# Attention score products as four 32-key column tiles, with the second half of the tokens reversed

## What is computed

```python
q = rope(h @ Wq)              # 32 heads of 64
k = rope(h @ Wk)              # 8 groups of 64, each shared by 4 heads
scores = q @ k.T              # per head, 256 queries x 256 keys
scores = (scores - slope * abs(i - j)) / 8
scores = 30 * tanh(scores / 30)
scores = where(j <= i, scores, -inf)       # causal
probs = softmax(scores)
ctx = probs @ v
x = x + ctx @ Wo + bo
```

## Time and profile before

| what | value |
|---|---|
| timed runs, median | 1184.27 us (1182.19, 1184.27 and one of 4972.99) |
| span of the profiled execution, first to last instruction | 1182.6 us |
| what lies around the span, by the median | 1.7 us |
| mean granted TensorE clock | 0.995 of full |
| PE busy | 1146.9 us (97%) |
| DVE, POOL, ACT busy | 877.6, 688.9, 554.0 us |
| attention stage, from the first scores to the last | 39.1 to 647.8 us |

### The profile page before, as it was taken

How to read it: one execution, slowest core, us unless ns; L and a number is a source line. 1 busy time by engine, 2 the same in 40 slices (tenths; PEclk the granted TensorE clock), 3 DMA queues, 4 the chain that set the end, 5 groups by cost and what they waited for, 6 DMA issues and landing times. The chain is left out here.

```text
span 1182.6 us, 24878 instructions
## 1 busy us (share of the span) xinstructions
PE 1146.9 (97%) x9715; PEld 794.2 (67%) x9730; DVE 877.6 (74%) x1287; ACT 554.0 (47%) x617; POOL 688.9 (58%) x557
## 2 busy tenths in 40 slices
PE   4888999999999999999999999999999999999998
PEld 4655556657657566566565677777886776786683
DVE  6879878787888787878887688889745745654654
ACT  6766565564755656647556400000244543542441
POOL 1454395784865957849659589999342422423331
PEclk9999999999999999999999999999999999999999
DMA  9563443554445335543455367772012022012000
GB/s 324 156 201 116 121 131 111 164 188 117 125 146 173 122 123 167 187 120 120 129 174 186 116 124 148 143 150 67 1 20 48 7 55 54 18 35 54 19 19 36
DMA packets 166142, 133.48 MB, mean 113 GB/s; under 512 B 69628, under 2 KB 127362, under 8 KB 166082
## 3 DMA queue, kind: packets, MB, share of 16 engines
q1 hardware_dynamic: 141128, 126.44, 36.3%
q10 hardware_dynamic: 24960, 6.29, 3.6%
HBM read 81.76 MB, written 35.21 MB: 99 GB/s over the span
## 5 line engine op out<-in xcount | busy, mean ns | idle before, releaser
L700 PE MATMUL bank<-hT_halves,w_hi 128*128 128x256 f16 x640 | 176.2, 275 | 5.4 <-DVE hT_halves L1419 3.6
L1973 POOL TENSOR_TENSOR parts<-parts 128x512 f32<-128x512 f32 x80 | 118.8, 1489 | 106.8 <-DVE parts L1435 106.8
L701 PE MATMUL bank<-hT_halves,w_hi 128*128 128x256 f16 x640 | 175.8, 275 | 0.0
L702 PE MATMUL bank<-hT_halves,w_lo 128*128 128x256 f16 x640 | 175.8, 275 | 0.0
L952 PE MATMUL bank<-kv,toep 128*128 128x288 f32 (+2 forms) x660 | 159.5, 404 | 0.7 <-ACT qT L1200 0.5
L1978 POOL TENSOR_SCALAR_AFFINE_SELECT region_c<-region_c 128x512 f32<-128x512 f32 x128 | 113.2, 908 | 63.5 <-ACT region_c L1166 63.3
L952 PEld LDWEIGHTS bank<-kv,toep 128*128 128x128 f32 x660 | 124.7, 192 | 34.4 <-ACT qT L1200 0.8
L2121 POOL TENSOR_TENSOR sqsum<-sqsum,toep 128x512 f32<-128x512 f32 x56 | 78.0, 1393 | 95.5 <-ACT toep L1342 95.3
L1991 POOL TENSOR_TENSOR ctx_lo<-ctx,ctx_hi 128x512 f16<-128x512 f32 x64 | 99.0, 1547 | 59.1 <-ACT ctx_hi L1142 59.1
L1163 ACT ACTIVATE region_c<-bank,cap_scale 128x1536 f32<-128x1536 f32 x64 | 98.7, 1542 | 74.2 <-PE bank L768 73.6
L1031 PE MATMUL bank<-odd_halves,guT 128*128 128x256 f16 x512 | 112.2, 273 | 0.0
(11 more groups left out here) (192 smaller groups left out, 2666.4 us busy)
## 6 DMA issues: line engine op xcount, KB each, us to landing
unit_halves<-halves SPq DMA_DIRECT2D x80, 256.0 KB, 2.2
q_both<-unit_halves SPq DMA_DIRECT2D x64, 256.0 KB, 2.9
q_high<-unit_halves SPq DMA_DIRECT2D x64, 128.0 KB, 3.0
toep<-kernel_padded SPq DMA_DIRECT2D x32, 256.0 KB, 3.9
wffn<-w_gu SPq DMA_DIRECT2D x6, 1280.0 KB, 6.2
cpair<-ctx_pairs SPq DMA_DIRECT2D x32, 176.0 KB, 4.8
xin<-x SPq DMA_DIRECT2D x8, 512.0 KB, 3.9
region_o<-wq SPq DMA_DIRECT2D x4, 1024.0 KB, 11.3
```

What stands on the lines that cost most here:

```text
L700: pe.matmul(dst, lh, rh, start=first and k == 0, stop=False)
L701: pe.matmul(dst, lh, rl, start=False, stop=False)
L702: mm = pe.matmul(dst, ll, rh, start=False, stop=last and k == n - 1)
L1973: pool.tensor_tensor(slot[:, 0], slot[:, 0], slot[:, 1], ALU.add).then_inc(unit_summed, 1)
```

## The change

Three things, all within `scores`, `mask` and the host's preparation.

1. Each bank is computed by four column tiles of 32 keys: tile c of a bank holds keys 32c to 32c + 31 of the bank's block and writes partitions 32c to 32c + 31. For each bank first the four high products are issued (L779 in the new numbering), then the four low ones (L781). That is 24 matmuls for a group where there were 6.
2. A tile takes only the queries that can see its keys. In banks 0 and 1 tile c takes the queries from 32c on: 512, 448, 384 and 320 columns for c = 0 to 3 (two heads). The rest of the bank holds what was there, is passed through tanh and exp as before, and is zeroed by the mask.
3. The last 128 tokens stand in reverse order everywhere (inputs, rotary tables, bias, context and output are permuted on the host). So in bank 2 the queries that can see a key stand before it, and tile c takes the first 32(c + 1) of them: 128, 256, 384 and 512 columns (four heads). Over the three banks each tile has 1152 columns in its high and 1152 in its low products. The mask of bank 2 has its signs turned.

Tiles are issued from c = 3 down to 0.

```diff
+KW = 32
...
-                def both(dst, t, heads, queries):
-                    keys = slice(t * P, (t + 1) * P)
-                    pe.matmul(dst, k_high[:, g, keys], q_both[:, heads, queries], start=True, stop=False)
-                    return pe.matmul(dst, k_low[biased, g, keys], q_high[biased, heads, queries], start=False, stop=True)
-
-                for n in range(2):
-                    both(bank[:, SC_BANKS[n], :], 0, slice(REP * g + 2 * n, REP * g + 2 * n + 2), slice(0, S))
-                both(bank[:, SC_BANKS[2], :], 1, slice(REP * g, REP * (g + 1)), slice(P, S)).then_inc(sc_filled, 1)
+                def score_tiles(n):
+
+                    for c in reversed(range(P // KW)):
+                        own, keys = slice(c * KW, (c + 1) * KW), slice(n // 2 * P + c * KW, n // 2 * P + (c + 1) * KW)
+                        if n < 2:
+                            yield (bank[own, SC_BANKS[n], :].rearrange("p (h s) -> p h s", h=2)[:, :, c * KW:], keys,
+                                   slice(REP * g + 2 * n, REP * g + 2 * n + 2), slice(c * KW, S))
+                        else:
+                            yield (bank[own, SC_BANKS[n], :].rearrange("p (h s) -> p h s", h=REP)[:, :, 0:(c + 1) * KW], keys,
+                                   slice(REP * g, REP * (g + 1)), slice(P, P + (c + 1) * KW))
+
+                for n in range(3):
+                    for dst, keys, heads, queries in score_tiles(n):
+                        pe.matmul(dst, k_high[:, g, keys], q_both[:, heads, queries], start=True, stop=False)
+                    for dst, keys, heads, queries in score_tiles(n):
+                        mm = pe.matmul(dst, k_low[biased, g, keys], q_high[biased, heads, queries], start=False, stop=True)
+                mm.then_inc(sc_filled, 1)
...
-                for s in (sc_first[:, g % 3, :, 0:P], sc_second[:, g % 3]):
-                    last = pool.affine_select(s, s, pattern=[[0, REP], [1, P]],
-                                              compare_op=ALU.is_ge, fill=0.0, base=0, channel_multiplier=-1)
+                for s, sign in ((sc_first[:, g % 3, :, 0:P], 1), (sc_second[:, g % 3], -1)):
+                    last = pool.affine_select(s, s, pattern=[[0, REP], [sign, P]],
+                                              compare_op=ALU.is_ge, fill=0.0, base=0, channel_multiplier=-sign)
...
+TOKENS = np.concatenate([np.arange(0, P), np.arange(S - 1, P - 1, -1)])
+HEADS = TOKENS[::HD] // HD
```

More of the change, by code:

```diff
@@ L2149, in _ @@
             inverse_rms(B - 1)
+TOKENS = np.concatenate([np.arange(0, P), np.arange(S - 1, P - 1, -1)])
+HEADS = TOKENS[::HD] // HD
 def shape_constants():
     inv_freq = (1.0 / np.float32(10000.0) ** (np.arange(0, DH, 2, dtype=np.float32) / np.float32(DH))).astype(np.float32)
-    freqs = inv_freq[:, None] * np.arange(S, dtype=np.float32)[None, :]
+    freqs = inv_freq[:, None] * TOKENS.astype(np.float32)[None, :]
     cos = np.repeat(np.cos(freqs).astype(np.float32), REP, axis=0) * np.float32(QK_DOWN)
@@ L2162, in pieces @@
         return [a, b, (v - a - b).astype(np.float16)]
-    at = np.arange(S, dtype=np.float64) - S // 2
+    at = TOKENS.astype(np.float64) - S // 2
     slopes = np.array(SLOPES, dtype=np.float64)[:, None] * BIAS_SCALE * np.ones(S)
@@ L2186, in by_halves @@
         return np.asarray(w).reshape(NG, REP, 2, SQ, D).transpose(0, 2, 1, 3, 4).reshape(NH * DH, D)
-    c = np.asarray(ctx_2048).reshape(B, HM, HD, LB, P).transpose(1, 4, 3, 0, 2)[:, ::-1]
+    c = np.asarray(ctx_2048)[:, TOKENS].reshape(B, HM, HD, LB, P).transpose(1, 4, 3, 0, 2)[:, ::-1]
     c = np.concatenate([c, c[..., 0:WRAP - HD]], axis=-1).reshape(HM, P, LB * B, WRAP)
@@ L2191 @@
     arrays = {
-        "x": x, "ctx_pairs": c, "wq": by_units(L0_attn_Wq), "wk": by_units(L0_attn_Wk), "wv": L0_attn_Wv, "wo": by_halves(L0_attn_Wo),
-        "bo": L0_attn_bo, "kern": L0_xattn_ssm_kernel, "dcoef": L0_xattn_D, "w_gu": L0_ffn_w_gate_up, "w_p": L0_ffn_w_proj,
+        "x": np.asarray(x)[:, TOKENS], "ctx_pairs": c, "wq": by_units(L0_attn_Wq), "wk": by_units(L0_attn_Wk), "wv": L0_attn_Wv, "wo": by_halves(L0_attn_Wo),
+        "bo": L0_attn_bo, "kern": np.asarray(L0_xattn_ssm_kernel)[HEADS], "dcoef": np.asarray(L0_xattn_D)[HEADS], "w_gu": L0_ffn_w_gate_up, "w_p": L0_ffn_w_proj,
         "rope_cos": cos, "rope_sin": sin, "key_bias": key_bias, "query_bias": query_bias, "ident": ident,
@@ L2201 @@
     r = run_bass_kernel_spmd(nc, [arrays], core_ids=[0])
-    return r.results[0]["out"]
+    return np.asarray(r.results[0]["out"])[:, TOKENS]
```

## The result

| | before | after |
|---|---|---|
| median | 1184.12 us (four runs, one of them 4972.99) | 1196.24 us (four runs, 1191.5 to 1199.93) |
| ratio to before, 95% interval | | 1.0107, 1.0075 to 1.0139 |
| span of the profiled execution | 1182.6 us | 1192.8 us |
| mean granted TensorE clock | 0.995 | 0.991 |
| first scores to first scores, batches 0 to 7 | 96.8, then 78.6 to 78.9 six times | 95.1, 80.5, 84.8, 81.1, 81.6, 80.1, 77.2 |

A forecast was written before the change was run, and what follows sets the result against it. PE was taken to bound the loop, with POOL's ctx_lo close behind. Gains of 3.6 us in the loop, 0.6 in batch 0 and 0.1 in batch 7 made 4.3, so 1180.0 us, range 1171 to 1187.

The forecast's parts named there:

- What is late next: Loop, other engines: their work stays; POOL's ctx_lo holds PE at step 7, leaving 0.60 us a batch.
- the sum for PE alone: PE's own gain from cheaper scores: 1.94 us a batch, 15.5 us over eight batches, the most possible.
- 1.00 us a group: Scores of a group on column tiles: four tiles overlap fully, 1.00 us instead of 1.30.
- issue order: Rival, scores: a tile's product waits until the one issued before has started; 1.11 us a group, 1181.6 us; chance 0.18.
- float16 tiles in each other's way: Slower rival, scores: four float16 streams can't run together; over 1.30 us a group, about 1222 to 1350 us; chance 0.08.
- slow weight loads: Scores: if a tile takes weights no faster than 0.11 us a pass, a group takes 1.09 us.
- 0.11 us in and 0.12 out between full array and tiles: PE's changes between full array and column tiles: 0.11 us going in, 0.12 us going back.
- PE busy down by about 14 us: Sign that the forecast is right: PE's busy time falls by about 14 us.
- A wait of 1.3 us for ctx_lo at step 7: Sign in each loop batch: PE newly waits about 1.3 us for POOL's ctx_lo before its step 7 filler.
- The small one at step 5: Loop batches: perhaps also a small new wait of PE for ctx_lo at step 5, no size given.
- 4.3 us in all: Whole kernel: 3.6 us from six loop batches, 0.6 from batch 0 and 0.1 from batch 7.
- 0.6 for batch 0: Batch 0, not bound by PE: 0.6 us gained of a possible 1.9, from scores on the queries' chain.

The follow-up runs named there:

- e8: Changed kernel with the value products left out in the loop as in e7, and the low score products of three of four tiles too; 1179.94 us, ratio 0.9974.
- e2: Changed kernel with PE's loop of batches 1 to 6 written out, so without jumps back; 1185.88 us, ratio 1.0024.
- e7: Kernel before, with only the first of four heads' second value products (keys 128 to 255) made in the loop; 1184.37 us, ratio 1.001.
- e3: Kernel before with PE's loop of batches 1 to 6 written out, so without jumps back; 1187.36 us, ratio 1.0033.
- e13: The kernel of e6 with its loop unchanged, but full score products in groups 0 to 2 of batch 0; 1199.24 us, ratio 1.013.
- e6: Changed kernel with column tiles in the loop only in groups 6 and 7, full score matmuls in the other groups; 1181.64 us, ratio 0.9987.
- e9: Changed kernel with, in the loop, tiles of 32 keys in groups 6 and 7, of 64 in group 5, full matmuls elsewhere; 1180.83 us, ratio 0.9979.
- e14: Changed kernel with, in the loop, tiles of 32 keys only in groups 5 to 7, and full products in group 0 of batch 0; 1181.89 us, ratio 0.9986.
- e4: Changed kernel with two column tiles of 64 keys instead of four of 32; 1208.66 us, ratio 1.0197.
- e10: The kernel of e9 with tiles of 64 keys in the loop's groups 4 and 5 too; 1207.56 us, ratio 1.0218.
- e12: The kernel of e10 with the same loop, but full score products in group 0 of batch 0; 1181.13 us, ratio 0.9987.
- e1: Kernel before with each full score product cut into four of 128 columns on the full array; 1202.61 us, ratio 1.0166.
- e15: Kernel before with its loop unchanged, but full score products of groups 0 to 3 of batch 0 cut into four; 1202.84 us, ratio 1.0177.

## Why the prediction was wrong, and what of it held

**The step that failed** is the sentence under "What is late next" that says "no DMA changes, so nobody else gets less to do", and with it the sum for PE alone, which priced PE's own 144 matmuls more a round by their columns. A DMA did change: the queue of PE's instructions went from no packet in the loop to 44, with five waits on issue, 11.6 us in all. That PE's instructions have to be brought, and that the loop was held at the engine until then, was no term of the sum and no rival. It could have been seen: the page of before gives the instruction queue 37 packets for the whole program, and the DMA view of the loop has none of them. What was lacking is a count of the loop's instructions and of the pieces they touch.

The account of the loop: six batches at the forecast's 78.1 us are 468.6, after took 485.3, so 16.7 more. In it are 11.6 us of waits on issue, 4.5 - 1.1 = 3.4 more for the halves, and four stretches at the lower clock at 1.7 us, 6.8: together 21.8. Back come about 5, since with PE that late its waits for ctx_lo are 3.1 us instead of the 8.1 of e8. That makes about 17 against 16.7. The fetch costs more than its own gap, by what follows it. That PE is late also means that after keeps more of the tiles' gain than the forecast gave it, and the 12 us are what is left of a larger loss.

Step by step:

- *1.00 us a group.* Held: 324.91 to 325.91. The rivals on issue order and on float16 tiles in each other's way (over 1.30) are out. The starts that the issue-order rival gave come out at 0, 0.14, 0.27, 0.43, 0.65 and 0.87 when its own rule is worked through, so its price is 1.09, not 1.11, the same as that of slow weight loads; 1.00 excludes both. The tiles of a group go on independently.
- *0.11 us in and 0.12 out between full array and tiles.* The way out held: the first product on the full array stands at 327.75, 0.32 behind the key sums at 327.43; in the earlier trace rows it is 0.34. The way in held too: the last full product starts at 324.60, and 324.91 is 0.09 more than its 0.217 us behind it, as in the earlier trace rows.
- *PE busy down by about 14 us.* It fell by 8.3 in after, where matmuls at the lower clock count as longer, and by 1146.9 - 1131.6 = 15.3 in e2, where all but one of those stretches are gone.
- *A wait of 1.3 us for ctx_lo at step 7.* Held: 1.1 us in every batch of e2 and e8, where no jump with a fetch stands ahead of it; in after it is 0.4 to 1.1 us, since PE comes late. The small one at step 5 that the forecast had as possible is there too (0.3 to 0.4 us in most batches of both), and the six batches of e8 are 78.1 us on the mean, as forecast.
- *4.3 us in all.* Held where the fetch is out: 4.4 us between e7 and e8, with all groups tiled. The intervals of the two leave nearly 2 us on either side, so that it meets 4.3 so closely is luck, and its 0.6 for batch 0 can't be told: from its own first scores to those of batch 1 that batch took from 94.3 us (e3) to 100.6 (e13), with no order by tiles. The kernels with two or three tiled groups (e6, e9, e14) also have batches of 78.1 to 78.3 us from the third of the loop on, and lie from 0.1 to 0.2% under before. That POOL holds PE back, so that more tiled groups would give no more, fits that.
- *The rivals and the range.* At 1.1% slower the result lies within 2% of before, as the chances had it, but outside the range, and no rival has its place or its price. The slower rival had the sign right and the mechanism wrong.

Why e4 and e10, with fewer instructions in a round, lose more than after (14.8 and 12.6 us more in the loop) can be read in part from their traces. After gains 0.30 us in most groups by its tiles, and with PE late that gain is not waited away. With tiles of 64 a group takes 1.22 us instead of 1.00, and the full groups of e10 gain nothing: an estimate from the time that each group takes, its changes of tile included, gives 9 and 7 us more of PE's own work in the six batches. The waits on issue add 3.2 and 2.5 us, those for the halves 4.0 and 5.1, and the 3.1 us of waits for ctx_lo in after are gone in both. Open is why these waits are longer, and why the fetch costs 28 us more in e10's loop than in e12's, which is the same, but only 14 more in e13's than in e6's.

Open too is what decides whether a gap is followed by the lower clock: in after it follows one of 2.04 us and not one of 2.24, and the loops of e1, e13 and e15 have one such stretch each where after has four.

Of the versions with all products e9 has the lowest median, 1180.83 us, 0.21% under before (0.07 to 0.35%), 15 us under the change as it was made; the intervals of e6, e12 and e14 overlap with its own.

## What to carry to other kernels

A long loop has a second size beside its work: its instructions on one engine, and the fetch pieces they touch. Count them before pricing a change that makes more, smaller instructions, and look in the DMA view whether the instruction queue runs while the loop does. Where "issue" stands once a round at the first instruction of the loop body, try moving the loop, or shortening it by a few instructions, before looking for a cause in the work, and let a control keep the loop's place too: an edit in batch 0 alone cost 20 us in a loop that it never touched (e15).

## What the runs showed of the hardware that I had not expected

- A loop that touches seven pieces of 256 instructions costs no fetch, one that touches eight costs between eight and nine packets a round, 1.7 to 3.3 us of idle at each jump back (1.7 in e15, 3.3 in e4), and what follows from it: 18 to 27 us between kernels whose loops are the same or differ in six matmuls. Six matmuls (e9 to e10) or nothing in the loop at all (before to e15) decide it.
- After some of these gaps the granted clock falls to 1.2 GHz for 3.4 us (0.53 in 296.90 to 300.30), although PE was fully busy up to the gap and again from 296.13 on.
- A score product can start before one that stands ahead of it in the program, if that one is on another tile. In the rows above L781 of 320 columns starts at 325.34 and L779 of 512 columns, which is issued ahead of it for the same bank, at 325.37. The first product of the third bank (L779, 512 columns, 325.48) starts 0.11 us ahead of the last low product of the second bank (L781, 512 columns, 325.59), which is issued before it. The Trainium skill, in "TensorE: Matmul & The Clock Gate", Part 3, says that matmuls keep program order; these rows don't show that for products on different column tiles.
- Instructions that are fetched once, in order, with no jump, bring no wait on issue (none in e2 and e3), but they are not free for the whole: 4 us in e3 (0.22 to 0.43%).
